# Gated recurrence: input projections of chunks 4 to 14 by seven block products in place of eight, and the gates' products no longer joined

## What is computed

```
x = x + layer0(x, cond)       # three projections, sigmoids, a scan over time
x = x + layer1(cond, x)
# layer 1:
vz, vr, vh = cond @ C_z + b_z, cond @ C_r + b_r, cond @ C + b
xz, xr, xh = x @ W_z, x @ W_r, x @ W         # for every step
for t in range(128):                          # h is 64 x 512, from zero
    z = sigmoid(xz[t] + h @ U_z + vz)
    r = sigmoid(xr[t] + h @ U_r + vr)
    hh = tanh(xh[t] + (r * h) @ U + vh)
    h = (1 - z) * h + z * hh                  # the output of step t
```

## Time and profile before

| | us |
|---|---|
| median of 3 runs | 1560.21 (1559.51 to 1560.81) |
| the profiled execution | 1560.92 |
| its span, first to last instruction | 1559.1 |
| first step with products (t = 1) to t = 24 | 184.6 |
| steps 24 to 111 (chunks 4 to 14 are projected) | 706.9 |

### The profile page before, as it was taken

The page is one execution under the profiler, slowest core; times in us unless marked ns, Lnnn a source line. Parts: engine busy times, 40 slices in busy tenths (PEclk is TensorE's granted clock), DMA queues, the critical chain, the costliest instruction groups (busy, mean ns, idle before and its releaser), DMA issues.

```text
span 1559.1 us, 47815 instructions
## 1 busy us (share of the span) xinstructions
PE 1547.6 (99%) x20030; PEld 1053.1 (68%) x20030; DVE 1371.0 (88%) x3244; ACT 826.0 (53%) x1819; POOL 264.3 (17%) x317
## 2 busy tenths in 40 slices
PE   8999999999999999999999999999999999999998
PEld 6875544444444467777777777777777777777998
DVE  6999889989999889888888888888888889888887
ACT  6989799999999733323333333333333333333333
POOL 0100111111110012112221211222122122211222
PEclk9999999999999999999999999999999999999999
DMA  5056355565548893761807618268083580800000
GB/s 192 28 156 214 86 154 147 131 163 145 156 107 133 106 76 36 29 51 8 56 31 28 52 7 56 38 21 56 2 57 41 18 56 8 51 29 2 30 31 31
DMA packets 538856, 109.91 MB, mean 70 GB/s; under 512 B 518288, under 2 KB 521616, under 8 KB 530320
## 3 DMA queue, kind: packets, MB, share of 16 engines
q1 hardware_dynamic: 534896, 79.58, 40.3%
q0 software_dynamic: 3744, 27.26, 9.2%
HBM read 61.75 MB, written 33.55 MB: 61 GB/s over the span
## 4 chain that ended last, share of the span: by engine, by line
PE 97%; DVE 2%; issue 1%; DMA 0%; ACT 0%; SPq 0%; DVEq 0%
PE ps L1059 32%; PE ps L1113 29%; PE ps L1141 17%; PE ps L1129 16%; PE ps L1077 2%; PE ps L1026 1%; DMA raw<-in_x 0%; DVE ST L937 0%; PE ps L1090 0%; DVE RL L969 0%; DVE XP L904 0%; DVE HL L991 0%; ACT ST L603 0%; DVE ST L997 0%; DVE ST L970 0%
## 5 line engine op out<-in xcount | busy, mean ns | idle before, releaser
L1059 PE MATMUL ps<-XH,WH 128*128 128x512 f16 x1872 | 404.7, 379 | 0.0
L1059 PEld LDWEIGHTS ps<-XH,WH 128*128 128x128 f16 x1872 | 183.2, 98 | 220.2 <-issue 0.3
L1113 PE MATMUL ps<-XB,W 128*128 128x512 f16 (+1 forms) x1584 | 272.4, 321 | 0.0
L1113 PE MATMUL ps<-AR,W 128*128 128x512 f16 x1008 | 235.8, 379 | 0.0
L1129 PEld LDWEIGHTS ps<-HL,U 128*128 128x128 f16 x6352 | 210.7, 98 | 28.2 <-issue 1.8
L1129 PE MATMUL ps<-HL,U 128*128 128x64 f16 x6352 | 226.8, 193 | 1.7 <-DVE HL L991 1.7
L1141 PE MATMUL ps<-HL,U 128*128 128x64 f16 x4064 | 207.5, 204 | 0.0
L599 ACT ACTIVATE ST<-ST 128x256 f32<-128x256 f32 x127 | 52.9, 417 | 264.1 <-DVE ST L942 238.2
L1113 PEld LDWEIGHTS ps<-XB,W 128*128 128x128 f16 x1584 | 126.6, 98 | 92.7
L1225 POOL TENSOR_TENSOR ST<-ST 128x256 f32<-128x256 f32 x127 | 92.4, 727 | 513.4 <-ACT ST L599 513.4
L1141 PEld LDWEIGHTS ps<-HL,U 128*128 128x128 f16 x4064 | 177.5, 98 | 0.1
(11 more groups left out here) (126 smaller groups left out, 2167.5 us busy)
## 6 DMA issues: line engine op xcount, KB each, us to landing
x_scratch<-AR SPq DMA_DIRECT2D x16, 1024.0 KB, 5.3
AR<-in_x POOLq DMA_DIRECT2D x15, 1024.0 KB, 8.2
AR<-HB POOLq DMA_DIRECT2D x11, 1024.0 KB, 7.1
raw<-x_scratch SPq DMA_DIRECT2D x11, 1024.0 KB, 21.6
out_y<-raw SPq DMA_DIRECT2D x11, 1024.0 KB, 4.0
raw<-in_x SPq DMA_DIRECT2D x10, 1024.0 KB, 7.5
ST<-in_x SPq DMA_DIRECT2D x5, 1024.0 KB, 7.6
out_y<-AR SPq DMA_DIRECT2D x4, 1024.0 KB, 5.6
```

The costliest lines, as they stand in the source:

```text
L1059: op = pe.matmul(ps[b][:, :], v[:, g, wp, k, e * P:(e + 1) * P], y[:, xp, k, :], start=n == 0, stop=n == 11)
L1113: op = pe.matmul(o, second_weights(W2_ORDER.index(g), wp, k, e), x, start=n == 0, stop=n == 11)
```

## The change

Chunks 4 to 14 (`by_seven`) are projected by Strassen's scheme in Winograd's form. The weights (512 x 512) and x1 (512 x 512 columns) are cut into 2 x 2 blocks; seven products of blocks take the place of eight, with sums of blocks as operands. The columns are halved by time: steps 0 to 3 and 4 to 7 of the chunk.

- **TensorE.** A turn is now one block product of a gate: 12 matmuls of 256 columns that fill one bank (two tiles e side by side). There are 21 turns in a chunk in place of 12, so 252 matmuls of 256 columns in place of 144 of 512, 31 or 32 in a step. `look` is 8 in place of 4 for them.
- **Sums of the results.** Some go through the banks: ScalarE writes V, scaled up, into the bank ahead of turn m=1 (`put_v`), and the difference of V's halves ahead of turn m=3 (`put` in `take`); the matmuls then add to it. Turns m=0 and m=4 are read out by ScalarE (`take`), m=0 into a buffer `Y1`. The other five turns of a gate are read out by VectorE, which adds Y1 or Y2.
- **Operands.** For x1 VectorE forms four sums of blocks per chunk (`x1_sum`, each two instructions of 256 columns) at tt 0 and 4, and seven blocks are split into halves (`x1_hi` on ScalarE at tt 0 to 6, `x1_lo` on VectorE one step later) in place of four tiles. For the weights four sums are formed and split, once for each gate, in steps 6 to 20, from copies that three new transfers of 1 MB bring.
- **Gates.** `is_joint` is now true for Z alone and only in steps below 16. Elsewhere a gate is 48 matmuls of 64 columns and one sum on VectorE.
- The scales of the splits leave room for the sums (a factor of 4). Layer 0 and chunks 1 to 3 and 15 are computed as before.

```diff
-JOINT = T - 2 * TC
-RESET = 1
+JOINT = 2 * TC
+QUICK = 4
+TURNS = 7
+SUMS = (6, 10, 14)
...
+        def bank_ready(i):
+            if of_seven(i, 1):
+                return s_prev, preloads(i, 1)
+            if of_seven(i, 3):
+                return s_predv, preloads(i, 3)
+            return (s_xa, xa_count[i - 3]) if by_act(i - 3) else (s_xp, xp_count[i - 3])
...
-            return LOOK if t < TC * (NCH - 2) else LAST_LOOK
+            j = t // TC
+            return LAST_LOOK if j >= NCH - 2 else 2 * LOOK if by_seven(j + 1) else LOOK
...
+        BLOCKS = (1, 0, 3, 4, 5, 2, 6)
+        SUM_ORDER = (3, 0, 6, 2)
...
-            return t < JOINT and g != RESET
+            return t < JOINT and g == 0
...
+            load_sw(0)
+            sp.wait_ge(s_mm[2], 4 * NCH)
+            load_sw(1)
...
+                    if j == 0:
+                        sp.wait_ge(s_swlo, KT)
+                        load_sw(2)
...
+            def put(i, v, done):
+                g = turns[i][1]
+                gi = W2_ORDER.index(g)
+                act.activation(by_4(ps[PB[i % 3]][:, :]),
+                               v.rearrange("p e b -> p (e b)").unsqueeze(2).to_broadcast([P, 2 * B, TC // 2]), ACT.Copy, scale=ux1[:, gi:gi + 1]).then_inc(done, 1)
+            def put_v(i):
+                act.wait_ge(s_ux1, 1)
+                act.wait_ge(s_xp, xp_count[i - 3])
+                put(i, V[:, turns[i][1], 0:2], s_prev)
+            def take(i):
...
+                act.wait_ge(s_prj, i + 1)
+                if m == 4:
+                    act.activation(xp_block(j, g, 0, 0), by_e(ps[PB[i % 3]][:, :]), ACT.Copy, scale=dx1[:, gi:gi + 1]).then_inc(s_xa, 1)
+                    return
+                if of_seven(i - 1, 6):
+                    act.wait_ge(s_xp, xp_count[i - 1])
...
+                act.activation(Y1, ps[PB[i % 3]][:, :], ACT.Copy, scale=dx1[:, gi:gi + 1]).then_inc(s_xa, 1)
+                act.wait_ge(s_xa, xa_count[i])
+                put(i + 3, DV[:, g], s_predv)
...
                         act.activation(two(rg, h), two(rg, h), ACT.Sigmoid).then_inc(s_r, 1)
+                    for i in done_second(t - 1):
+                        if of_seven(i + 3, 1):
+                            put_v(i + 3)
+                    for i in done_first(t):
+                        if by_act(i):
+                            take(i)
                     act.wait_ge(s_pz, u + 1)
...
                 act.activation(hn[t % 2], Hst[t % 2], ACT.Copy, scale=1.0 / HS).then_inc(s_hn, 1)
-                if 2 <= tt < 6 and j + 2 < NCH:
+                for i in done_second(t):
+                    if by_act(i):
+                        take(i)
+                if by_seven(j + 2):
+                    if tt < TURNS:
+                        x1_hi(j + 2, tt)
+                elif 2 <= tt < 6 and j + 2 < NCH:
                     x1_hi(j + 2, tt - 2)
...
                 evacuate_second(t)
-                if 3 <= tt < 7 and j + 2 < NCH:
+                if by_seven(j + 2):
+                    if tt == 4:
+                        x1_sum(j + 2, 6)
+                    if tt:
+                        x1_lo(j + 2, tt - 1)
+                    for m in {0: (3, 0), 4: (2,)}.get(tt, ()):
+                        x1_sum(j + 2, m)
+                elif 3 <= tt < 7 and j + 2 < NCH:
                     x1_lo(j + 2, tt - 3)
...
+                for i in range(3):
+                    if 0 <= t - SUMS[i] < 2:
+                        sw_sums(i, t - SUMS[i])
+                    if 3 <= t - SUMS[i] < 3 + KT:
+                        sw_lo(i, t - SUMS[i] - 3)
...
+            def seven(i, n):
+                j, g, m = turns[i]
+                gi = W2_ORDER.index(g)
+                (wp, xp), e, k = PRODUCTS[n // 4], n % 4 // 2, n % 2
...
+                w = SW[gi] if m in (0, 2, 3, 5) else W2[:, gi]
+                kk, ee = {0: (0, 0), 1: (0, 0), 2: (1, 1), 3: (0, 1), 4: (1, 0), 5: (1, 0), 6: (1, 1)}[m]
+                ee = 2 * ee + e
+                op = pe.matmul(ps[PB[i % 3]][:, e * 256:(e + 1) * 256], w[:, wp, 2 * kk + k, ee * P:(ee + 1) * P],
+                               blocks_of(j, m)[1][:, xp, k], start=n == 0 and m in (0, 2), stop=n == 11, skip_group_check=True)
```

More of the change, by code:

```diff
@@ L256, in build, with by_seven, turn, products_of @@
         R, C, Z, PB = (0, 1), (2, 3), 4, (5, 6, 7)
-        def fills(j, part=None):
-            return [(j, part, g, e, n % KT, *PRODUCTS[n // KT], n) for g in W2_ORDER for e in range(KT) for n in range(3 * KT)]
+        def by_seven(j):
+            return QUICK <= j < NCH - 1
+        turns = []
+        for j in range(1, NCH - 1):
+            turns += [(j, g, m) for g in W2_ORDER for m in range(TURNS if by_seven(j) else KT)]
+        turns += [(NCH - 1, g, part) for part in range(PARTS) for g in W2_ORDER]
+        def turn(j, g, m):
+            return turns.index((j, g, m))
+        def products_of(i):
+            return 3 * KT * (KT if turns[i][0] == NCH - 1 else 1)
+        def of_seven(i, *ms):
+            return 0 <= i < len(turns) and by_seven(turns[i][0]) and turns[i][2] in ms
+        def turns_of(j):
+            return [i for i in range(len(turns)) if turns[i][0] == j]
+        def by_act(i):
+            return of_seven(i, 0, 4)
+        xp_count, xa_count = [], []
+        for i in range(len(turns)):
+            xp_count.append((xp_count[-1] if i else 0) + (0 if by_act(i) else 2 if turns[i][0] == NCH - 1 else 1))
+            xa_count.append((xa_count[-1] if i else 0) + by_act(i))
+        def preloads(i, m):
+            return sum(of_seven(n, m) for n in range(i + 1))
+        def bank_ready(i):
[4 more added lines that the diff above has]
+            return (s_xa, xa_count[i - 3]) if by_act(i - 3) else (s_xp, xp_count[i - 3])
         def fills_of_step(t):
@@ L887, in _, with evacuate @@
                 evacuate_b(n)
-            def evacuate(j, part, g, e, step=None):
-                i = number(j, part, g, e)
+            def evacuate(i, step=None):
+                j, g, m = turns[i]
                 if i == 0:
@@ L897, in evacuate @@
                 gi = W2_ORDER.index(g)
[L898 to L903 removed]
+                p = ps[PB[i % 3]][:, :]
@@ L904, in evacuate, with in_parts @@
                 dve.scalar_tensor_tensor(out=out, in0=src, scalar=dx1[:, gi:gi + 1], in1=v,
                                          op0=ALU.mult, op1=ALU.add).then_inc(s_xp, 1)
-            def complete(items):
-                return [(j, part, g, e) for j, part, g, e, k, wp, xp, n in items if n == 11 and (part is None or e == KT - 1)]
+            def in_parts(i):
+                return turns[i][0] == NCH - 1
             def evacuate_first(t):
-                late = complete(fills_of_step(t - 1)[look(t - 1):]) if t else []
-                for j, part, g, e in [b for b in late if b[1] is not None] + complete(fills_of_step(t)[:look(t)]):
-                    evacuate(j, part, g, e, 0)
+                for i in [n for n in done_second(t - 1) if in_parts(n)] + done_first(t):
+                    if not by_act(i):
+                        evacuate(i, 0)
@@ L916, in evacuate_second @@
             def evacuate_second(t):
-                late = complete(fills_of_step(t - 1)[look(t - 1):]) if t else []
-                for j, part, g, e in late + complete(fills_of_step(t)[:look(t)]):
-                    if part is not None:
-                        evacuate(j, part, g, e, 1)
-                for j, part, g, e in complete(fills_of_step(t)[look(t):]):
-                    if part is None:
-                        evacuate(j, part, g, e)
+                for i in done_second(t - 1) + done_first(t):
+                    if in_parts(i):
+                        evacuate(i, 1)
@@ L925, in add_x @@
+                for i in done_second(t):
+                    if not in_parts(i) and not by_act(i):
+                        evacuate(i)
             def add_x(t, dst, b, g, es, s_high, s_done, count):
```

225 lines of the change are left out of this document (179 added, 46 removed).

## The result

The changed kernel takes 1596.86 us (median of 4, 1594.09 to 1599.94), the kernel before on the same chip 1559.86: ratio 1.0237, 95% interval 1.0215 to 1.026. It is slower by 37 us; the forecast was 22 us faster.

The account below looks back on a forecast made before the run. The prediction took TensorE, busy 99%, to bound the kernel, with VectorE having little room. It summed 1560.9 - 35.5 + 1.2 + 4.2 + 5.0 + 2.2 = 1538.0 and said 1538 us, range 1526 to 1554.

Parts of the forecast that it names:

- TensorE's gain: Steps 24 to 111: step of 7.63 us against 8.033, with fills at 109.1 ns, so -35.5 us.
- How early VectorE is in an unjoined step: VectorE behind `hlo`: 1.51 us of extra work fit without delay, 2.52 us without a stall of TensorE.
- V into the bank at tt 3: ScalarE's `put_v` behind r's sigmoids comes late for its bank; stall 0.50 a chunk, +5.0 us.
- The heavy end of tt 4: VectorE's work behind `hlo` at tt 4 exceeds the cover; 0.42 of stall in ten chunks, +4.2 us.
- Weights' sums: VectorE's sums and splits of weights, steps 6 to 20, exceed the cover in steps 11, 14, 15, 20; +2.2 us.
- The last 16 steps are the same instructions: Steps from 112 to the end: unchanged at 6.49 us, difference 0.
- the places of least margin give too: Rival: ScalarE's work before z and behind the state costs TensorE 0.35 in four more steps a chunk; 1553 us, chance 0.22.
- Bank handovers: Rival: each of six puts a chunk stops TensorE by 0.8 us, adding 53; 1579 us, chance 0.06.

Follow-up runs that it names:

- e12: Kernel before with the gates' products unjoined (Z joint only below step 16) and the x1 load in four pieces; 1565.14 us, ratio 1.0037.
- e3: Changed kernel with the gates' sums reading 64 columns in a row, no stride, so the output is not the reference's; 1570.23 us, ratio 1.007.
- e14: e11 with x1's block sums moved from VectorE to GpSimd, behind its add to the output; 1557.01 us, ratio 0.9986.
- e11: e6 with `put_v` moved to the end of the step before and x1's last block sum from tt 4 to tt 5; 1563.81 us, ratio 1.0028.
- e6: Changed kernel with each x1 load in the loop cut into four of 256 KB, issued one or two steps apart; 1576.99 us, ratio 1.0109.
- e13: e11 with plain reads of the projection (64 columns in a row, output not the reference's); 1535.71 us, ratio 0.9849.
- e7: Changed kernel, VectorE's order alone: two block sums ahead of m=1's evacuation at tt 0, last block sum from tt 4 to tt 5; 1591.30 us, ratio 1.02.
- e4: Changed kernel with x1 loads bringing the same bytes in runs of 2 KB, not 32 bytes (output not the reference's); 1577.20 us, ratio 1.0113.
- e10: Changed kernel with reads-out into the projection as two instructions of 256 writing at a 64-word stride, so the sums read in a row; 1595.79 us.

## Why the prediction was wrong

- **TensorE's gain: right.** 256 columns at 109.1 ns (measured 109.2), a step of 7.63 (88 steps of 671.1 without stalls, 671.4 forecast), unjoining 0.04 a gate (e12: steps of 8.09). The 81 and 131 ns that the prediction cites from the Trainium skill, "TensorE: Matmul & The Clock Gate", section "Back-to-back issue gap", do not hold here: 55.7 and 215.7 before, and 109.2 between them after.
- **The step that failed first: "How early VectorE is in an unjoined step".** It took the sums' durations from the last sixteen steps and left out that `xx` is read with a stride of four words, which stood in the diff. Four sums of 0.1 more and one of 0.19 more are 0.57 us a step. It breaks into the argument twice: the chain to `rhi` and `rlo`, and the room for extra work. An estimate from rows: 4.95 for VectorE's fixed chain (a step of 8.18 in step 60 with three extra pieces of 0.66, less the joint sums), 2.24 for the average extra and 0.57 make 7.76 a step, more than the 7.63 of TensorE, and without the 0.57 it is 7.19. What it cost: 26.6 us (e3). The average is not all of it: e14 takes 0.35 a step off VectorE, and 21.6 of e11's 30.1 us behind r*h stay, so where in the chunk the work lies counts too.
- **Missing altogether: TensorE without instructions.** 19.9 us (e6): in steps 24 to 111 25 us of pauses went and 8 us behind banks, hidden until then, came out; the rest is in the steps before 24. The forecast weighed the new loads' bytes and semaphores, not what the old long load does to an engine that takes a third more instructions a step (175.5 products in 7.6 us, before 130 in 8.0). It looked for waits only, and the trace of before had none of this kind.
- **"V into the bank at tt 3": right in place and size for its inputs** (0.50 forecast, 0.48 in chunk 3), 1.1 in the chunks with the longer sums. e11 removes it.
- **"The heavy end of tt 4": right in place, 0.42 forecast,** 0.52 in chunk 3, 1.47 with the strided sums.
- **Not asked: what the evacuation at tt 0 waits for.** It needs ScalarE's read, 0.61 us of VectorE. The stalls at tt 1 are 9.3 us, of which 4.4 remain with plain reads (e3; 4.3 in e13). How much of that is this wait no run shows, since e7 replaced it by a collision with GpSimd.
- **Weights' sums:** the steps after 11, 14, 15 and 20 were named; they cost 1.55, 1.19, 1.05 and 0.63 in place of 1.0, 0.35, 0.35 and 0.5 (e4, read without the second kind of stall). Steps 8, 14 and 17, not named, cost 0.23, 0.32 and 0.30 more. That lateness carries over from one step to the next is the likely reason; it was not tested.
- **"The last 16 steps are the same instructions": wrong by 1 us.** Chunk 14 is read with the stride; eight steps of about 6.62 in place of 6.49. One step of 6.72 in the kernel before is 6.49 now, so the total shows 0.7.
- **The rivals.** The one nearest to the truth was that the places of least margin give too, but it had 15 us for a miss of 59, and ScalarE's new work as its cause, where VectorE's was it. Bank handovers, the slower rival, were a small part: 3 to 10 us. With the strided reads away, the x1 load in four, and the put and the last block sum moved, e13 comes to 1536, near the forecast's 1538. That is in part luck: e11's moves removed the two stalls that were forecast, and others (6.1 us) were left.

Still open: that the stalls without a wait are late instructions is read from their place, from the transfers of instructions that end before each of them does, and from what removes them (runs of 2 KB, or pauses in the load). No run changed the transfers of instructions themselves. A layout that gives VectorE rows without a price elsewhere was not found; a copy of each step's columns by GpSimd was not tried.

## What to carry to other kernels

When a change alters a layout, follow it to every instruction that reads it, also those whose lines hardly change, and take their durations only from rows with the same stride. Where the busy engine's step is made shorter, here by a twentieth, the next engine's work per step has to be added up whole, with its lateness carried from step to step, before single stalls are priced. And more, smaller instructions need to arrive: look at what long transfers of small packets run beside them, and at the queue of instructions in the trace; cut the long transfers into pieces with pauses.

## What the hardware showed unexpectedly

- VectorE's sum of 128 words a partition, one operand from a bank and one from SBUF: 0.343 us in a row, 0.439 with a stride of four words; of 256, 0.479 and 0.670. Written to SBUF with a stride of 64 words, 256 take 0.67 (e10).
- TensorE with an f16 operand read at a stride of 8 bytes: 227 ns for 256 columns in place of 109. The Trainium skill's section on SBUF named above would let two accesses to the same 16-byte line go at full speed, and here two f16 lie in each; that did not hold. Results written 256 bytes apart into the bank: 216 ns. That agrees with the Trainium skill, "PSUM — Partial Sum Buffer", section "Specifications (TRN2)", which calls patterns that are not contiguous significantly slower.
- TensorE stood still up to 2.7 us without a semaphore to wait for, beside a load of 32768 packets of 32 bytes; four loads of a quarter, with pauses, had no such effect.
- Transfers of 16384 bytes on the instruction queue, one for some 254 instructions of TensorE, took 1.0 us, and 2.1 in the middle of such a load.
- VectorE's pair of sums of 256 took 1.41 in place of 0.75 us beside one GpSimd instruction (e7).
